# Perceiver kernel, one core: the last 65 tokens' keys and values move to a first stage of their own, and the first attention's key tiles become three of 512 columns

## The reference, cut to what matters

```python
q = (query @ Wq + bq).reshape(B, L, NKV, G, HDIM)        # B 8, L 64, NKV 8, G 4, HDIM 128
k_, v_ = jnp.split(kv @ Wkv + bkv, 2, axis=-1)           # kv: 8 x 1601 x 512, Wkv: 512 x 2048
scores = jnp.einsum('blkgd,bmkd->bkglm', q, k) * scale
attn = jax.nn.softmax(scores, axis=-1)
o = jnp.einsum('bkglm,bmkd->blkgd', attn, v).reshape(B, L, NHEAD * HDIM)
return o @ Wo + bo
```

## Time and profile before

| | |
|---|---|
| median of 3 runs (lowest, highest) | 2637.67 us (2636.87, 2637.9) |
| profiled execution, its own time | 2636.26 us |
| its span, first to last instruction | 2634.5 us |
| PE busy | 96% of the span, 17424 matmuls |
| DVE, ACT, POOL busy | 65%, 57%, 50% |
| mean granted TensorE clock | 0.978 |

### The profile page before, as it was taken

One profiled execution on the slowest core, in us unless ns is written; L12 is line 12 of the kernel. 1 busy time (PEld: TensorE's weight loads), 2 busy tenths in 40 slices (PEclk: granted clock), 3 DMA queues, 4 the chain that ended last, 5 costly groups with the idle time before them and its releaser, 6 DMA issues. The chain is left out here.

```text
span 2634.5 us, 43104 instructions
## 1 busy us (share of the span) xinstructions
PE 2522.5 (96%) x17424; PEld 2322.2 (88%) x17424; DVE 1725.3 (65%) x1970; ACT 1493.8 (57%) x2617; POOL 1305.0 (50%) x941
## 2 busy tenths in 40 slices
PE   7999999999999999999999999999999599899878
PEld 6899999999999999999999999999987377654557
DVE  2276677666777766776667777667656699743473
ACT  3365566655566655666555666556543577523572
POOL 1454654584475556448546455754600599300352
PEclk9999999999999999999999999999999699999899
DMA  5410111011011101101101100100351300187200
GB/s 202 160 50 25 50 50 41 25 58 50 29 62 50 33 24 51 66 25 50 58 25 56 60 25 27 56 25 27 105 178 53 128 1 1 65 299 244 90 1 17
DMA packets 99533, 173.91 MB, mean 66 GB/s; under 512 B 8114, under 2 KB 65714, under 8 KB 97546
## 3 DMA queue, kind: packets, MB, share of 16 engines
q1 hardware_dynamic: 91018, 162.81, 18.5%
q10 hardware_dynamic: 8320, 8.39, 0.9%
HBM read 153.28 MB, written 17.89 MB: 65 GB/s over the span
## 5 line engine op out<-in xcount | busy, mean ns | idle before, releaser
L458 POOL TENSOR_TENSOR xa_pt_lo<-xs_st,xa_pt_hi 128x1024 fp32r<-128x1024 f32 x255 | 508.2, 2027 | 564.1 <-ACT xa_pt_hi L667 564.1
L54 PE MATMUL ctx_kv_ps<-ctx_wv_hi,ctx_hi 128*128 128x256 f32 (+1 forms) x1664 | 467.5, 281 | 0.0
L56 PE MATMUL ctx_kv_ps<-ctx_wv_hi,ctx_lo 128*128 128x256 f32 (+1 forms) x1664 | 466.3, 280 | 0.0
L55 PE MATMUL ctx_kv_ps<-ctx_wv_lo,ctx_hi 128*128 128x256 f32 (+1 forms) x1664 | 466.0, 280 | 0.0
L54 PE MATMUL ctx_kv_ps<-ctx_hi,ctx_wk_hi 128*128 128x402 f32 (+1 forms) x1024 | 358.3, 350 | 2.3 <-DVE xa_k_lo L767 2.3
L55 PE MATMUL ctx_kv_ps<-ctx_lo,ctx_wk_hi 128*128 128x402 f32 (+1 forms) x1024 | 353.9, 346 | 0.0
L56 PE MATMUL ctx_kv_ps<-ctx_hi,ctx_wk_lo 128*128 128x402 f32 (+1 forms) x1024 | 353.1, 345 | 0.0
L776 DVE TENSOR_TENSOR xa_v_lo<-ctx_kv_ps,xa_v_hi 128x512 fp32r<-128x512 f32 (+1 forms) x224 | 146.3, 653 | 260.0 <-ACT xa_v_hi L640 259.4
L55 PEld LDWEIGHTS ctx_kv_ps<-ctx_wv_lo,ctx_hi 128*128 128x128 f32 (+1 forms) x1664 | 307.0, 185 | 0.0
L54 PEld LDWEIGHTS ctx_kv_ps<-ctx_wv_hi,ctx_hi 128*128 128x128 f32 (+1 forms) x1664 | 305.8, 184 | 0.0
L56 PEld LDWEIGHTS ctx_kv_ps<-ctx_wv_hi,ctx_lo 128*128 128x128 f32 (+1 forms) x1664 | 305.7, 184 | 0.0
(11 more groups left out here) (474 smaller groups left out, 6225.0 us busy)
## 6 DMA issues: line engine op xcount, KB each, us to landing
ctx_raw<-in_ctx_t SPq DMA_DIRECT2D x24, 804.0 KB, 6.7
ctx_wk_raw<-in_xa_wk SPq DMA_DIRECT2D x64, 256.0 KB, 2.9
ctx_wv_raw<-in_xa_wv SPq DMA_DIRECT2D x32, 512.0 KB, 4.4
n_back<-in_ctx SPq DMA_DIRECT2D x8, 1280.0 KB, 10.5
q_raw<-in_xa_wq SPq DMA_DIRECT2D x8, 1024.0 KB, 6.3
q_scratch<-q_q_sb ACTq DMA_DIRECT2D x8, 1024.0 KB, 4.4
ctx_q_raw<-q_scratch SPq DMA_DIRECT2D x64, 128.0 KB, 2.7
o_scratch<-xa_o_sb SPq DMA_DIRECT2D x64, 128.0 KB, 1.7
```

What stands on the lines that cost most here:

```text
L54: nc.tensor.matmul(out, left[0], right[0], start=first, stop=False)
L55: nc.tensor.matmul(out, left[0], right[1], start=False, stop=False)
L56: return nc.tensor.matmul(out, left[1], right[0], start=False, stop=last)
L458: nc.gpsimd.tensor_tensor(by_chunk(pt_lo, p), scored(j, p).rearrange("p g q c -> p g c q"), by_chunk(pt_hi, p).bitcast(F32), ALU.subtract) ...
```

## The change

The keys and values of each batch's last 65 tokens (8 x 65 = 520 rows) are made in a new stage, `context_rest`, that takes the place of `layernorm_transposed`, and go to DRAM (`k_scratch`, `v_scratch`). The layer norm of `x` is done in it too, between the heads. The keys are 8 heads x 2 tiles of 260 columns x 12 matmuls, the values 2 x 5 chunks of 104 rows x 12 matmuls of 512 columns. SP's transfers at its start are, in this order: head 0's key weights, the 520 context rows in four, biases, two more heads' key weights, `x` and the identity, the value weights, the first query weights; the key weights of head 3 come after all these.

In the attention the context that is held and split is 1536 tokens: three key tiles of 512 columns, and 12 value chunks in 6 tiles. The keys and values of the last 65 tokens are fetched from DRAM, keys for each unit, values for each pair, and split by POOL (`rest_keys`, `rest_values`). The orders of PE, ACT and DVE are rewritten for three key tiles.

```diff
 class Context:
-        self.SE = self.S + self.S % 2
-        self.TILES = even_tiles(self.SE)
+        self.S = S // P * P
+        self.TILES = even_tiles(self.S)
...
 @block.sync, cross_attention
+            def rest_keys(b, j):
+                n = unit(b, j)
+                if n >= 2:
+                    sp.wait_ge(rest_k_split, n - 1)
+                sp.dma_start(rest_k[:, n % 2], rest.k_dram[j % NKV, :, b + j // NKV]).then_inc(rest_k_in[n % 2], 16)
+            def rest_values(b, j):
+                n = unit(b, j) // 2
+                ...
+                if n >= 1:
+                    sp.wait_ge(rest_v_split, n)
+                sp.dma_start(rest_v[0:r, :], rest.v_dram[j % NKV // 2, at:at + r]).then_inc(rest_v_in, 16)
...
+                if has_keys(j, last):
+                    rest_keys(b, j + 1)
                 store(b, j - 1)
+                if j % 2 == 0:
+                    rest_values(b, j)
                 if j == NKV - 2 and not last:
                     for t in range(2, NT):
                         sp.wait_ge(ctx_lo_set, b * NT + NT + t - 1)
                         context.load(sp, b + 1, t)
...
 @block.gpsimd, cross_attention
+            def rest_keys(b, j):
+                pool.wait_ge(rest_k_in[n % 2], (n // 2 + 1) * 16)
+                pool.wait_ge(s_full, n * NG)
+                split_on_pool(nc, pool, k_hi[:, at], k_lo[:, at], rest_k[:, n % 2], rest_k_hi, n + 1
+                              ).then_inc(rest_k_split, 1)
+            def rest_values(b, j):
+                pool.wait_ge(rest_v_in, (n // 2 + 1) * 16)
+                pool.wait_ge(o_full, n + 1)
+                split_on_pool(nc, pool, v_hi[0:r, NC - 1, :], v_lo[0:r, NC - 1, :], rest_v[0:r, :], rest_v_hi,
+                              n // 2 + 1).then_inc(rest_v_split, 1)
...
             def group(b, j, last):
                 if not last or j + 2 < NKV:
                     key_weights(b, j + 2)
+                if j % 2 == 0:
+                    rest_values(b, j)
+                if has_keys(j, last):
+                    rest_keys(b, j + 1)
...
 @block.tensor, cross_attention: scores waits for rest_k_split before chunk 12, attend for rest_v_split
             def group(b, j, last, alone=False):
                 scores(b, j)
                 if j % 2:
                     attend(b, j - 1, lambda: turn_maxima(b, j))
+                    key_tile(b, j + 1, 0)
+                    spread_maxima(b, j)
+                    for t in range(1, NT):
+                        key_tile(b, j + 1, t)
+                    return
+                for t in range(NT):
+                    key_tile(b, j + 1, t)
+                turn_maxima(b, j)
+                attend(b, j - 1, lambda: spread_maxima(b, j), 1)
+                for g in range(NV):
+                    value_tile(b, j, g)
...
 @block.scalar, cross_attention, odd group
                     exponential(b, j, 0)
                     key_tile(b, j + 1, 1)
                     exponential(b, j, 1)
+                    exponential(b, j, 2)
                     key_tile(b, j + 1, 2)
-                    exponential(b, j, 2)
                     exponential(b, j, 3)
-                    key_tile(b, j + 1, 3)
...
+def context_rest(nc, scope, x_sb, ident, xt_hi, xt_lo, rest, context, early, arrival, first_weights, spare, plain,
+                 load_weights):
...
+            key_weights(0)
+            for k in range(KC):
+                sp.dma_start(r_raw[:, k, :], rest.ctx_r[:, k, :]).then_inc(r_in[k], 16)
...
+            load_weights(sp, 0)
+            for h in range(NKV):
+                if h + SLOTS < NKV:
+                    sp.wait_ge(wk_lo_set, h + 1)
+                    key_weights(h + SLOTS)
+                store_keys(h)
...
+            for h in range(NKV):
+                for t in range(NT):
+                    keys(h, t)
+                if TURN <= h < TURN + RT:
+                    norm.turn(pe, h - TURN)
+            for n in range(NV * NCH):
+                values(n)
```

More of the change, by code:

```diff
@@ L261, in cross_attention @@
     NU = NQ // P
-    SE, TILES = context.SE, context.TILES
+    TILES = context.TILES
     NC = -(-S // P)
     NG = -(-NC // 2)
+    NV = context.S // P // 2
     NT = len(TILES)
@@ L338, in cross_attention @@
         o_out = output.o_out
+        rest_k, rest_v = sc.sb("rest_k", [P, 2, S - context.S]), sc.sb("rest_v", [P, 2 * D])
+        rest_k_in = [sc.sem(f"rest_k_in{i}") for i in range(2)]
+        rest_v_in, rest_k_hi, rest_v_hi, rest_k_split, rest_v_split = (
+            sc.sem(n) for n in ("rest_v_in", "rest_k_hi", "rest_v_hi", "rest_k_split", "rest_v_split"))
         block = sc.block()
@@ L514, in value_tile @@
                 pe.wait_ge(kv_free, b * KV_TILES + n + 1)
-                for c in range(2 * g, min(2 * g + 2, NC)):
+                for c in range(2 * g, 2 * g + 2):
                     for kc in range(KC):
-                        s = slice(c * P, c * P + rows(c))
+                        s = slice(c * P, c * P + P)
                         o = (c % 2) * 2 * D
-                        end = product(nc, kv_ps[0:rows(c), n % 2, o:o + 2 * D],
+                        end = product(nc, kv_ps[:, n % 2, o:o + 2 * D],
                                       (ctx_hi[:, kc, s], ctx_lo[:, kc, s]),
@@ L701, in first_unit @@
                 sum_high(b, j)
-                for g in range(3, NG):
+                for g in range(3, NV):
                     value_tile(b, j, g)
@@ L731, in group @@
                     high(b, j, 3)
-                    for g in range(1, NG):
+                    for g in range(1, NV):
                         value_tile(b, j, g)
@@ L875, in group @@
                     key_tile(b, j + 1, 2)
-                    shifted(b, j, 0)
-                    key_tile(b, j + 1, 3)
-                    for p in range(1, NP):
+                    for p in range(NP):
                         shifted(b, j, p)
@@ L885, in group @@
                     summed_in_two(b, j, 1)
-                    for g in range(2, NG):
+                    for g in range(2, NV):
                         value_tile(b, j, g)
@@ L893, in group @@
                     normalise(b, j - 1)
-                    for p in range(NP):
-                        shifted(b, j, p)
-                        key_tile(b, j + 1, p)
+                    shifted(b, j, 0)
+                    key_tile(b, j + 1, 0)
+                    shifted(b, j, 1)
+                    key_tile(b, j + 1, 1)
+                    shifted(b, j, 2)
+                    shifted(b, j, 3)
+                    key_tile(b, j + 1, 2)
                 else:
@@ L1127, in low_rest, with __init__ @@
         self.nc.vector.tensor_tensor(lo, raw, hi.bitcast(F32), ALU.subtract).then_inc(self.lo_set, 1)
-def queries(nc, x_sb, ident, xt_hi, xt_lo, wq, bq, q_dram, context, early, arrival):
+class ContextRest:
+    def __init__(self, nc, scope, ctx_r, k_dram, v_dram):
+        self.ctx_r, self.k_dram, self.v_dram = ctx_r, k_dram, v_dram
+        self.N = ctx_r.shape[2]
+        self.TILES = even_tiles(self.N)
+        self.CHUNKS = -(-self.N // P)
+        self.STEP = -(-self.N // self.CHUNKS)
+        self.k_out, self.v_out = ([scope.sem(f"{n}_out{i}") for i in range(2)] for n in "kv")
@@ L1132, in queries @@
+def queries(nc, x_sb, ident, xt_hi, xt_lo, wq, bq, q_dram, context, early, rest, arrival):
     NKV, _, KC, GD = wq.shape
@@ L1148, in queries, with load @@
         first_weights = FirstWeights(nc, sc, raw[:, 0], w_hi[:, 0], w_lo[:, 0], w_in[0], w_hi_set, w_lo_set)
-        def load(sp):
-            arrival.load(sp)
-            for i in range(2):
-                sp.dma_start(raw[:, i], wq[i]).then_inc(w_in[i], 16)
-            sp.dma_start(bq_sb[:, :], bq).then_inc(bias_in, 16)
-        layernorm_transposed(nc, "q_ln", x_sb, xt_hi, xt_lo, ident, load, arrival.prepare, arrival, first_weights)
+        def load(sp, i):
+            sp.dma_start(raw[:, i], wq[i]).then_inc(w_in[i], 16)
+            if i == 0:
+                sp.dma_start(bq_sb[:, :], bq).then_inc(bias_in, 16)
+        context_rest(nc, sc, x_sb, ident, xt_hi, xt_lo, rest, context, early, arrival, first_weights,
+                     [raw[:, 1], w_hi[:, 1], w_lo[:, 1]], q_sb[:, :, :, :, :].rearrange("p s b g l -> p (s b g l)"), load)
         q_ps = sc.ps("q_ps", [P, 4, 512])
@@ L1175, in _ @@
                 context.load(sp, 0, t)
+            for i in range(2):
+                sp.wait_ge(rest.k_out[i], rest.k_dram.shape[0] // 2 * 16)
+                sp.wait_ge(rest.v_out[i], NKV * D // 512 * rest.CHUNKS // 2 * 16)
             early.load(sp)
@@ L3429 @@
     }
+    ctx_t = i["ctx_4096"].transpose(0, 2, 1).reshape(B, H // P, P, S).swapaxes(1, 2)
     alone = {
```

364 lines of the change are left out of this document (228 added, 136 removed).

## The result

The changed kernel takes 2683.03 us (median of 4 runs, 2681.95 to 2684.93) where the kernel before takes 2637.27 beside it (4 runs, 2636.45 to 2637.9): a ratio of 1.0175, 95% interval 1.016 to 1.019. That is 45.8 us more, where 29 were forecast; 2683 lies inside the range. The profiled execution took 2683.09 us.

A forecast was written before the change was run, and what follows sets the result against it. The prediction took PE as the bound, never waiting in the attention. Gains of 88.2 us against losses of 52.4, 48.3, 13.4 and 3.1 gave +29.0 on 2637.67, so 2667 us, range 2614 to 2694.

The forecast's parts named there:

- keys: PE's attention keys: three 512-column tiles take 36 x 0.2262 = 8.14 us a unit instead of 8.81; 64 units gain 42.9 us.
- values: PE's attention values: the chunk of 65 tokens goes, 1.415 us in each of 32 pairs; 45.3 us gained.
- first stage: New stage before the queries: first query matmul at 70.1 us instead of 17.7, with 4 us waiting for head 3's weights; +52.4.
- change of batch: Attention: late rest_v delays POOL's context splits, PE waits for two key tiles, clock falls; 6.9 us x 7 = +48.3.
- odd groups' order: ACT's order in odd groups delays the first copy of the next scores; PE waits 0.56 us in 24 groups, +13.4.
- spread and first unit: Even groups' spread of the maxima waits 0 to 0.1 us x 32, +1.6; the very first unit +1.5; together +3.1.
- queries to first scores: Stage following the new first one: paced by PE as before, one context tile less to split; no cost in the sum.
- Rival D: More comes late (rest_k of head 0, head 3's weights, later heads): 2690 us; the page's narrower pace ends here too; chance 0.13.
- Rival B: Change of batch costs nothing, third tile in time if splits start by 12.5 us: 2619, or 2605 without ACT wait; chance 0.15.

The follow-up runs named there:

- experiment 7: Changed kernel with the early weights allocated ahead of the context, so both lie at other SBUF addresses: 2681.16 us, ratio 1.0168.
- experiment 12: Changed kernel with rest_v's transfer before the store, VectorE's third shift earlier, first-stage transfers reordered, plus key weights 64 bytes lower in SBUF: 2600.08 us.
- experiment 6: Changed kernel with SP's first-stage transfers reordered by due time (key weights of heads 3 to 5, then stores of heads 0 and 1 first): 2674.04 us.
- experiment 1: Changed kernel with SP issuing the transfer of rest_v ahead of the store of the head before it: 2639.96 us, ratio 1.0011.
- experiment 2: Changed kernel with POOL's splits of rest_v and rest_k behind its low halves and sum_low in even groups, SP's order kept: 2643.18 us.
- experiment 3: Changed kernel with VectorE's third shift ahead of the low half of key tile 1 in odd groups: 2671.31 us, ratio 1.0135.
- experiment 5: Changed kernel with the spread of the maxima behind the attend's second piece instead of its first, in even groups: 2710.64 us, ratio 1.0274.

## Why the prediction was right, and what of it was not

The sign and the mechanisms were right, and the time in range; one term was mis-sized by 15 us, which is nearly the whole distance to 2683. By its own steps, measured in the two profiled executions (means over all units of a kind, from start to start; "change of batch" is a whole odd group at the 7 places against one elsewhere). The spans differ by 46.5 us, and the terms sum to that within 0.1:

| step | forecast | measured |
|---|---|---|
| keys | -42.9 | 64 x (8.84 - 8.40) = -28.2 |
| values | -45.3 | 32 x (18.39 - 16.94) = -46.4 |
| first stage | +52.4 | 72.88 - 17.78 = +55.1 |
| change of batch | +48.3 | 7 x (25.13 - 18.27) = +48.0 |
| odd groups' order | +13.4 | 32 x (5.03 - 4.61) = +13.4 |
| spread and first unit | +3.1 | 31 x 0.17 + 1.5 = +6.8 |
| queries to first scores, without the keys' gain | 0 | 99.75 - 102.24 + 0.4 = -2.1 |

- *Keys, the step that failed:* "36 x 0.2262", the pitch of the query's 512-column matmuls (from start to start it is 0.2267: 373 matmuls start in those 84.60 us, and the row's count has one that started before them). The kernel's own key matmuls started 4.42 / 24 = 0.1842 us apart at 402 columns, 16.7 ns over the columns at 2.4 GHz, where the query's had 12.9 at 512. The line from 0.1179 at 256 columns through 0.1842 at 402 gives 0.234 at 512, which is what came. That line is no law: experiments 7 and 12 have the same key matmuls at 0.2278 with other addresses, so that at 512 columns the difference to the query's was made by where the operands lie. Whether the 402-column pitch came about in the same way was not tried.
- Rival D had in it the narrower pace of the Trainium skill ("TensorE: Matmul & The Clock Gate", "Wait — 56ns, not 53.3ns?"), by which 512 columns would start every 0.2158 us, an estimate. The trace has 0.2336, wider and not narrower.
- *First stage:* the last context quarter was there at 8 to 9, and PE had heads 0 to 2 done at 17.9 and not 20, so that its wait for head 3 (at 24.0 as forecast) was 6.1 us and not 4. The matmuls behind it started 0.22 us apart until 28.1, and from there 0.12. Experiment 6 shows both as avoidable.
- *Change of batch:* place, order, landing and size as forecast (2.0 us for the 65 KB, taken as 2.3). Five of the seven cost 6.3 to 6.5 us. The other two cost 7.6 and 8.4, since the clock stayed low longer there (a mean granted clock of 0.57 and 0.61 over the 8 us from 830 and from 1278, against 0.79 over the 8 us from 386). That the sum comes within 0.3 of the forecast is in part luck. Experiments 1 and 2 give 43 and 40 us back and so show the cause. Rival B's point, splits from 12.5, fits the 0.5 us left in experiment 2.
- The estimate for the landing by the Trainium skill ("DMA: Bandwidth & Descriptors", "Anatomy of one DMA — SWDGE (gpsimd) path", 2.15 us), whose section is on transfers that GpSimd issues, comes near the trace of this one, which SyncE issued: 354.17 to 356.15, 1.98 us. It does not fit the others of that queue as well: 1.7 and 2.7 us for 128 KB, where the estimate by it is 2.3, and 3.9 us (median) for the 32.5 KB of `rest_k` in the changed kernel, where it is 2.1.
- *Odd groups:* 24 groups as forecast, of 0.53 us each between starts (forecast 0.56); experiment 3 gives 11.7 back.
- *Spread:* forecast 1.6 us. From the attend's start to the values' start it is 5.18 us in place of 4.89, 0.12 of it the spread itself, so 0.17 in each of 31 groups. Half of it, 0.08, is lost at the spread, which is followed by the next matmul after 0.20 us and not 0.12; experiment 5 took that away. The other half is no new loss. The first matmul behind the turning is followed by the next only after 0.20 us here (343.97 to 344.17), and before the change that matmul was the fourth key tile's, so that the same kind of loss (0.29 in place of 0.18) stood in the 8.84 of the keys:

```profile
293.55 0.45 PE L54 MATMUL ctx_kv_ps<-ctx_hi,ctx_wk_hi 128*128 128x396 f32 x1
293.84 0.34 PE L55 MATMUL ctx_kv_ps<-ctx_lo,ctx_wk_hi 128*128 128x396 f32 x1
```

- *First unit:* it cost 1.5 us between starts, as forecast, 1.2 of them idle.

## What to carry to other kernels

Price a new shape by the pitch of the matmuls that it replaces, with the same operands, at two widths, and not by another stage's of the right width. Where a transfer is waited for in an engine's written order, what counts is the work behind the wait: 7 us of lateness were harmless in 24 pairs and cost 6.9 us each at the 7 places where a chain of splits stood behind, and moving one issue ahead of a store, or the wait behind the work, ended that. And before a step is moved by 1.4 us, list every bank and slot that is freed behind it, in its engine's order and in the order of each engine that follows it.
